# Sigmoid rounding of the first feed-forward: from VectorE to GpSimd, with four buffers

## The reference

```python
def act_qdq(x):
    qmax = 2.0 ** (ACT_BITS - 1) - 1.0
    scale = jnp.maximum(jnp.max(jnp.abs(x)) / qmax, 1e-12)
    return jnp.clip(jnp.round(x / scale), -qmax - 1.0, qmax) * scale

def fixed_qdq_u16(x):
    scale = 1.0 / 65536.0
    return jnp.clip(jnp.round(x / scale), 0.0, 65535.0) * scale
...
x = act_qdq(x)
up = act_qdq(x @ lpbq_dequant(w_up).T)
gate = act_qdq(x @ lpbq_dequant(w_gate).T)
sig = fixed_qdq_u16(jax.nn.sigmoid(gate))
gate = act_qdq(gate * sig)
o = act_qdq(gate * up)
return o @ lpbq_dequant(w_down).T
```

## Time and profile before

| what | us |
|---|---|
| median of 3 runs | 1942.84 (1941.39 to 1942.87) |
| the profiled execution | 1938.02 |
| its span, first to last instruction | 1936.2 |
| TensorE busy in the span | 1690.7 (87%) |
| VectorE busy | 1581.4 (82%) |
| ScalarE busy | 1505.8 (78%) |
| GpSimd busy | 837.8 (43%) |

### The profile page before, as it was taken

How to read it: one execution, slowest core, us unless ns; L and a number is a source line. 1 busy time by engine, 2 the same in 40 slices (tenths; PEclk the granted TensorE clock), 3 DMA queues, 4 the chain that set the end, 5 groups by cost and what they waited for, 6 DMA issues and landing times. The chain is left out here.

```text
span 1936.2 us, 50375 instructions
## 1 busy us (share of the span) xinstructions
PE 1690.7 (87%) x13527; PEld 1332.0 (69%) x13527; DVE 1581.4 (82%) x5121; ACT 1505.8 (78%) x4166; POOL 837.8 (43%) x1319
## 2 busy tenths in 40 slices
PE   3699999999999999996540789999999799889997
PEld 3588888888888888873330656666666566577775
DVE  4898888888888888867779689999999688776664
ACT  3688888888888888866696599999999598764553
POOL 2654444444444444422220034444444277725554
PEclk8699999999999999998575899999999799969999
DMA  5366666666666666650000079999999600024555
GB/s 160 101 169 168 167 167 164 161 166 165 168 164 162 164 164 167 167 138 1 1 1 0 24 187 251 250 249 249 244 248 248 156 17 0 1 46 98 94 97 106
DMA packets 230623, 263.89 MB, mean 136 GB/s; under 512 B 26712, under 2 KB 183932, under 8 KB 230416
## 3 DMA queue, kind: packets, MB, share of 16 engines
q1 hardware_dynamic: 229062, 260.81, 54.3%
q10 hardware_dynamic: 1194, 1.58, 0.3%
q0 software_dynamic: 288, 0.56, 0.1%
HBM read 90.35 MB, written 4.74 MB: 49 GB/s over the span
## 5 line engine op out<-in xcount | busy, mean ns | idle before, releaser
L839 PE MATMUL a_out<-a_probT,a_xn 128*128 128x256 f32 x1024 | 265.9, 383 | 3.8 <-DMA a_probT<-a_blocks 2.2
L759 ACT ACTIVATE a_prob<-a_neg,a_nmax 128x289 f32<-128x289 f32 x512 | 266.6, 524 | 1.3 <-DVE a_nmax L658 1.0
L1806 ACT ACTIVATE b_prob<-b_neg,b_nmax 128x257 f32<-128x257 f32 x512 | 260.0, 514 | 5.3 <-DVE b_nmax L1741 4.7
L611 POOL TENSOR_TENSOR a_xn<-a_z,g 128x256 f32<-128x256 f32 x128 | 94.5, 738 | 379.4 <-DVE a_z L700 379.4
L829 PE MATMUL a_score<-a_xnT,a_qT 128*128 128x290 f32 x1536 | 241.4, 306 | 1.2 <-DVE a_qT L711 1.1
L658 DVE CUSTOM_DVE_ANT_0 a_neg<-a_score,a_bias 128x289 f32<-128x289 f32 x512 | 208.3, 455 | 39.3 <-PE a_score L829 34.7
L829 PEld LDWEIGHTS a_score<-a_xnT,a_qT 128*128 128x128 f32 x1536 | 210.9, 189 | 42.7 <-issue 42.7
L767 ACT ACTIVATE a_prob<-a_prob,a_rinv 128x289 f32<-128x289 f32 x512 | 232.5, 528 | 9.2 <-DVE a_rinv L716 6.1
L1741 DVE CUSTOM_DVE_ANT_0 b_neg<-b_score,b_bias 128x257 f32<-128x257 f32 x512 | 188.4, 419 | 24.5 <-PE b_score L1911 17.0
L839 PEld LDWEIGHTS a_out<-a_probT,a_xn 128*128 128x128 f32 x1024 | 177.3, 193 | 19.0 <-DMA a_probT<-a_blocks 3.8
L675 DVE STREAM_TRANSPOSE a_blocks<-a_prob 128x1024 f32<-128x1024 f32 x128 | 159.3, 1244 | 13.4 <-ACT a_prob L767 9.1
(11 more groups left out here) (469 smaller groups left out, 4412.7 us busy)
## 6 DMA issues: line engine op xcount, KB each, us to landing
a_probT<-a_blocks SPq DMA_DIRECT2D x512, 192.0 KB, 3.5
b_probT<-b_blocks SPq DMA_DIRECT2D x256, 256.0 KB, 4.7
a_raw<-in_ctx SPq DMA_DIRECT2D x128, 128.0 KB, 3.0
b_raw<-in_ctx SPq DMA_DIRECT2D x64, 256.0 KB, 4.5
m_wide<-expert_weights SPq DMA_DIRECT2D x128, 128.0 KB, 7.2
a_kept<-keep SPq DMA_DIRECT2D x32, 257.0 KB, 3.5
b_kept<-keep SPq DMA_DIRECT2D x32, 257.0 KB, 4.9
b_v_rows<-ctx_tail_values SPq DMA_DIRECT2D x32, 256.0 KB, 4.7
```

The source lines that it names most:

```text
L759: nc.scalar.activation(prob[:, par, grp, 0:KEYS0], neg[:, grp, :], ACT.Exp, bias=nmax[:, par, grp:grp + 1], scale=-1.0, accum_out=rsum[:, ...
L839: nc.tensor.matmul(out_ps[:, half, 0:2 * P], xn[:, j, kt, :], probT[:, u, :, kt, half * (P // 2):(half + 1) * (P // 2)], start=(kt == 0), ...
L1806: nc.scalar.activation(prob[:, (j + 5) % 4, grp, :], neg[:, par, grp, :], ACT.Exp, bias=nmax[:, par, grp:grp + 1], scale=-1.0, accum_out=r ...
```

## The change

The rounding of the sigmoids moves from VectorE to GpSimd, behind GpSimd's loop over `y`, with the same semaphores around it. `part` has four buffers instead of three, so that sigmoid n waits for product n-4 and no longer for product n-3. VectorE's loop is product n, then maximum n-1.

```diff
@@ -1175,7 +1175,7 @@
     nc = k.nc
     W = 2 * CH
     ITEMS = FB0 * TOK // W
-    SLOTS = 3
+    SLOTS = 4
     SIG = 192.0
     SIG_MAX = SIG + 65535.0 / 65536
     with ExitStack() as stack:
@@ -1341,6 +1341,10 @@
                     pool.wait_ge(y_clean, c)
                     nc.gpsimd.tensor_tensor(y[:, LO, c * CH:(c + 1) * CH], chunk(yT, c), y[:, HI, c * CH:(c + 1) * CH], ALU.subtract)\
                         .then_inc(y_lo, 1)
+                for n in range(ITEMS):
+                    sig = part[:, n % SLOTS, :]
+                    pool.wait_ge(sig_ready, n + 1)
+                    nc.gpsimd.tensor_scalar(sig, sig, SIG, SIG_MAX, ALU.add, ALU.min).then_inc(sig_rounded, 1)
 
             @block.vector
             def _(dve):
@@ -1413,11 +1417,6 @@
                     nc.vector.tensor_reduce(ug_max[:, at:at + FB0], t[:, :, c * CH:(c + 1) * CH], AX.X, ALU.max,
                                             apply_absolute_value=True).then_inc(maxed, 1)
 
-                def round_sigmoid(n):
-                    sig = part[:, n % SLOTS, :]
-                    dve.wait_ge(sig_ready, n + 1)
-                    nc.vector.tensor_scalar(sig, sig, SIG, SIG_MAX, ALU.add, ALU.min).then_inc(sig_rounded, 1)
-
                 def multiply_gate(n):
                     dve.wait_ge(sig_rounded, n + 1)
                     nc.vector.scalar_tensor_tensor(item(all_gate, n), part[:, n % SLOTS, :], -SIG, low(item(all_gate, n)), ALU.add, ALU.mult)\
@@ -1473,10 +1472,7 @@
                 dve.wait_ge(maxed, 2 * CHUNKS)
                 find_scale(UG, ug_max[:].rearrange("p (t c) -> p t c", t=2))
 
-                round_sigmoid(0)
                 for n in range(ITEMS):
-                    if n + 1 < ITEMS:
-                        round_sigmoid(n + 1)
                     multiply_gate(n)
                     if n > 0:
                         max_gate(n - 1)
```

## The result

The change made the kernel slower. The median of 6 runs is 1950.66 us, beside 1940.6 for the kernel before in 6 runs, 10.06 us apart. The ratio of the runs is 1.0048 (95% interval 1.0036 to 1.0060), which is some 9 us, 7 to 12 by the interval. I had forecast 1940.4 with a range of 1938.0 to 1943.0, and called slower by more than 0.2% a case of 5 in 100.

What follows compares the result with a forecast made beforehand. VectorE was taken to bound the gate stretch by its backlog over ScalarE. With the rounding on GpSimd the last reduction moves from 1033.65 to 1031.17, 2.5 us off the median 1942.84: forecast 1940.4 us, range 1938.0 to 1943.0.

Steps and rivals of the forecast that it cites:

- the price of GpSimd's rounding: Gate stretch: one rounding of 1024 columns on GpSimd taken as 1.05 us, range 0.98 to 2.54.
- Rival 3: Gate stretch: dear rounding and product exclude each other, slower from 1.58 us a rounding; 1948.8 at 2.08, 1954.3 at 2.54; chance 0.05.
- exclusion: SBUF access: GpSimd's rounding and VectorE's product take turns, 1.05 + 0.11 + 1.21 = 2.37 us an item.
- VectorE's backlog over ScalarE: Gate stretch: VectorE at 2.87 us an item lags ScalarE at 2.74; only this lag, at product 10, can be won.
- rival 2: Gate stretch: VectorE alone is the bound and all twelve roundings count, 7.2 us saved, 1935.6; chance 0.02.
- the collision: End of gate stretch: rounding 11 starts 0.12 us before product 10 is asked for and holds it off until 1026.78.
- rival 1: End of gate stretch: rounding 11 doesn't hold product 10 off, 3.3 us saved, 1939.6; chance 0.23.
- the sum: Gate stretch, first scaling to next stage's scaling: 40.8 us instead of 43.26, 2.5 us saved.
- hand-over from GpSimd to VectorE: Gate stretch: VectorE starts 0.11 us after the GpSimd instruction it waits for ends.
- the 0.2 us that GpSimd was to wait: Between the other items of the gate stretch: GpSimd waits some 0.2 us for a running product, which is hidden.
- the fourth buffer: Gate stretch: a buffer more takes 0.12 us off the start of sigmoid 11, worth nothing by itself.
- Rival 4: Whole kernel: the change does nothing, some other wait sets the end, 1942.8; chance 0.07, including a gain taken back elsewhere.

Runs made afterwards that it cites:

- The probe: Kernel before plus a stage computing nothing of the result, timing GpSimd instruction forms alone and beside VectorE; multiply-and-add took 1.047 us, every other pair tried 3.63.
- e8: Changed kernel with rounding as multiply by 1, add 192 (no minimum), plus a second quick GpSimd instruction per item; stretch 44.70 us against 43.26 before.
- the kernel of the multiply-and-add: Changed kernel with GpSimd's rounding as multiply by 1 and add 192, minimum left out; stretch 40.77 us, ratio to before 0.9985.

## Why the prediction was wrong

**The step that failed** is the price of GpSimd's rounding: "The nearest row is the same instruction with bf16 input and two arithmetic steps, 128x1028, 1.05 us", and from it "I take 1.05, as one input is read. Range 0.98 to 2.54". It measured 3.63, 1.43 times the upper end. The row was of the same opcode and shape, but of another pair of operations: line 1688 multiplies and adds, the change adds and takes a minimum. I had weighed the input's type, the number of inputs and the columns, and not which operations the instruction carries. The probe varied the input's type, VectorE's company and the operations, and of these only the operations moved the price: for the pair of line 1688 the row's price was right to the hundredth (1.047). The upper end came from doubling instructions on two tensors, which the prediction calls additions though line 1110 of the earlier trace rows multiplies. It priced them fairly (the probe's product and sum of two tensors at 128x1024 take 2.34), but they say nothing about an add-and-minimum either.

The trace of before held a warning. Two groups by form, both GpSimd scalar operations on a few columns (shapes, count, busy us, mean ns, idle before):

```profile
L617 POOL TENSOR_SCALAR a_var<-a_mv 128x2 f32<-128x2 f32 x128 | 28.7, 224 | 0.0
...
L636 POOL TENSOR_SCALAR a_bias<-a_kept 128x4 f32<-128x4 bf16 x32 | 6.6, 207 | 0.0
```

Line 617 adds, line 636 multiplies and adds. Half the columns and one operation less took longer. That is a small difference, and the input types differ too, but it has the wrong sign for a cost that goes by elements.

**Rival 3** had the right sign and mechanism, and its point of decision, 1.58 us, was passed; it had 5 in 100 because its price stopped at 2.54. Its formula was wrong too, in the other direction. At 3.63 it gives 1012.42 + 12 x 3.63 = 1055.98 for product 11, 24.6 us later than 1031.39, and measured were 9.1. It charges a product's 1.21 on top of every rounding, because the prediction took exclusion to last for a whole instruction. In fact the slow rounding keeps a product off only at its start: product 3 (items count from 0) starts at 1012.30, right behind the start of rounding 4 at 1012.24, and ends 2.05 later, 0.84 more than its own 1.21, while the rounding goes on for another 1.5 us. So GpSimd's own 3.59 an item is the bound, and the e8 kernel, at two quick instructions an item, loses 1.44 us where the formula gives some 7 for 2.2 an item.

**Confirmed once the price is put right**, by the kernel of the multiply-and-add: that VectorE's backlog over ScalarE is what can be won and not 12 x 0.60 (rival 2 falls); that no backlog forms; that the collision comes at product 10 alone, and rival 1 falls; the sum, 40.77 against 40.8. Only the hand-over from GpSimd to VectorE was 0.03 us and not 0.11 (998.47 + 1.05 to 999.55 in its timeline), which the collision hid. And the 0.2 us that GpSimd was to wait for running products did not come: rounding 1 starts at 1000.64, 0.14 before product 0 ends, and lasts 1.05 as the others do. Neither moved the sum, by luck and not by working. That the fourth buffer is worth nothing by itself is confirmed in both kernels. Rival 4 falls too: what comes behind the stretch moves with it, and the stretch that follows has 30.81 us in every kernel here. One chance was added up wrongly: a fifth of the forecast's and rival 1's 0.86, with rival 2's 0.02, makes 0.19 for "faster", not 0.16.

On the two pages of the Trainium skill: "SBUF — State Buffer", section "Who interferes with whom", calls the shared pair an exclusive lock, and says that the one that issues first gets it "for the whole instruction". For the quick form the runs agree (product 10 at 2.08 us). For the slow form the measurement differs and decides: the product ends before the rounding does. "GPSIMD Engine Reference", section "Elementwise — side-by-side cycle accounting", gives bodies of up to two operations 1.03 cycles an element; at its 1.2 GHz that is an estimate of 0.86 ns. The 0.82 ns of the multiply-and-add come near it. The 3.3 ns of the other pairs and the 2.77 us of a single operation do not.

## What to carry to other kernels

A row prices an instruction only if it has the same engine, shape, types and operations. Where the trace has the opcode but another pair of operations, the cost is unknown, and on GpSimd that was a factor of 3.5. Time the very form alone before moving work onto it. When work moves from the bound engine to an idle one, ask what the idle one may cost at most: here each rounding had to fit into ScalarE's 2.74 us an item. And look at the order once more afterwards: VectorE's maximum ahead of the product and ScalarE's late last sigmoid were worth another 1.7 us (40.84 to 39.11).

## What the runs showed of the hardware

- GpSimd's scalar operation on 128x1024: multiply-and-add 1.05 us, also with bf16 input or with uint16 output; a single addition or minimum 2.77; every other pair tried 3.63. Why the single addition is dearer than the pair that contains it, no run shows.
- A slow GpSimd operation disturbs VectorE's product of two SBUF tensors only at its start. Timeline of the probe stage, two additions on GpSimd beside such products:

```profile
1235.73 1.22 DVE L1636 SCALAR_TENSOR_TENSOR p_d<-p_s,p_g 128x1024 f32<-128x1024 f32 x1
1235.79 4.67 POOL L1610 TENSOR_SCALAR p_a<-p_a 128x1024 f32<-128x1024 f32 x1 [0.21 <-DVE p_d L1633]
1236.99 3.20 DVE L1636 SCALAR_TENSOR_TENSOR p_d<-p_s,p_g 128x1024 f32<-128x1024 f32 x2
```

The first product came first, and the GpSimd operation lasts 1.04 us more than its 3.63, about the product's time. The second product lasts 1.94 (the longest of its line, 1941 ns), and the third 1.22 again, while the same GpSimd operation still runs until 1240.46.
- VectorE's fp32 scalar operation, from one SBUF tensor to another, lasts 0.69 us alone. Beside a slow GpSimd operation it is held off at the start and again near the end. Timeline of the probe stage, add-and-minimum on GpSimd until 1317.14:

```profile
1312.71 4.43 POOL L1608 TENSOR_SCALAR p_a<-p_a 128x1024 f32<-128x1024 f32 x1 [0.21 <-DVE p_d L1633]
1313.39 1.41 DVE L1640 TENSOR_SCALAR p_d<-p_s 128x1024 f32<-128x1024 f32 x1
...
1314.83 0.69 DVE L1640 TENSOR_SCALAR p_d<-p_s 128x1024 f32<-128x1024 f32 x1
...
1316.29 1.40 DVE L1640 TENSOR_SCALAR p_d<-p_s 128x1024 f32<-128x1024 f32 x1
```

The same pattern comes beside two additions. So "only at its start" holds for the product of two tensors and not for every VectorE instruction. Why they differ, no run shows.
- Reductions last 1.22 us beside slow operations in the probe and beside the quick one in the kernel, as alone.
